# Deformable convolution before a state-space scan: the offset convolution in two halves, GpSimd's copies moved, output rows turned in the layer norm

## The reference, cut to what matters

```python
x = x + conv_ref(_gn(x), offset_w, offset_b, weight, bias)
t = _to_tokens(x)
t = t + ssm_ref(_ln_t(t), ...)
t = t + ffn_ref(_ln_t(t), ...)

def conv_ref(x, offset_w, offset_b, weight, bias):
    offsets = conv2d(x, offset_w, offset_b, PAD)          # 18 channels: dy and dx of 9 taps
    ys = (row - PAD) + kh + dy
    xs = (column - PAD) + kw + dx
    sampled = bilinear_sample(x, ys, xs)                  # a tap's value at a fractional place
    out = jnp.einsum('bkhwc,ock->bohw', sampled, w)
    return out + bias[None, :, None, None]
```

## Time and profile before

| | us |
|---|---|
| median of 3 executions | 323.08 |
| lowest, highest | 322.18, 323.83 |
| the profiled execution's own time | 324.19 |
| its span, first to last instruction | 322.4 |

### The profile page before, as it was taken

One profiled execution on the slowest core, in us unless ns is written; L12 is line 12 of the kernel. 1 busy time (PEld: TensorE's weight loads), 2 busy tenths in 40 slices (PEclk: granted clock), 3 DMA queues, 4 the chain that ended last, 5 costly groups with the idle time before them and its releaser, 6 DMA issues. The chain is left out here.

```text
span 322.4 us, 5895 instructions
## 1 busy us (share of the span) xinstructions
PE 254.4 (79%) x2341; PEld 149.2 (46%) x2341; DVE 245.2 (76%) x193; ACT 218.9 (68%) x327; POOL 170.1 (53%) x103
## 2 busy tenths in 40 slices
PE   7698999999797324387679666978599897888893
PEld 2345777776452000034347335644486764255530
DVE  0349999990458899999999999999999983216731
ACT  1047777776267749999999999999996442434541
POOL 1330000000184939999999999999998970000000
PEclk9988999999999555559875996597858999599998
DMA  5300000000003000000000000000000000000001
GB/s 164 129 0 2 2 0 2 2 2 2 0 18 81 0 18 0 1 2 0 2 1 2 2 2 0 0 3 2 1 2 2 2 2 0 3 19 0 0 0 33
DMA packets 2638, 4.07 MB, mean 13 GB/s; under 512 B 691, under 2 KB 1844, under 8 KB 2612
## 3 DMA queue, kind: packets, MB, share of 16 engines
q1 hardware_dynamic: 2480, 3.58, 3.8%
q10 hardware_dynamic: 132, 0.13, 0.1%
HBM read 2.66 MB, written 0.26 MB: 9 GB/s over the span
## 5 line engine op out<-in xcount | busy, mean ns | idle before, releaser
L830 DVE TENSOR_TENSOR_SCAN pool<-ps,pool 128x1024 f32<-128x1024 f32 x63 | 143.7, 2288 | 4.3 <-POOL pool L454 1.3
L454 POOL TENSOR_TENSOR pool<-pool 128x1024 f32<-128x1024 f32 x58 | 135.0, 2350 | 11.3 <-DVE pool L830 5.3
L1115 PE MATMUL ps<-pool,picks 96*128 96x512 bf16 x120 | 50.5, 515 | 45.3 <-DVE pool L830 45.3
L581 ACT ACTIVATE ps<-ps,a_cols 128x1020 f32<-128x1020 f32 x64 | 69.5, 1085 | 8.2 <-DVE pool L807 4.7
L571 ACT ACTIVATE pool<-ps 128x1024 f32<-128x1024 f32 x58 | 59.2, 1020 | 11.3 <-PE ps L1115 8.5
L516 ACT ACTIVATE pool<-ps 128x1024 f32<-128x1024 f32 x36 | 34.9, 1024 | 13.4 <-PE ps L1007 13.4
L279 DVE TENSOR_TENSOR pool<-pool 128x2048 f32<-128x2048 f32 x18 | 40.5, 2287 | 1.3 <-ACT pool L497 0.9
L1137 PE MATMUL ps<-pool 128*32 128x112 f32 x1024 | 39.6, 293 | 0.0
L417 POOL MEMSET pool<- 128x4096 f32 x1 | 3.5, 3512 | 68.2 <-DVE tn L719 68.2
L1115 PEld LDWEIGHTS ps<-pool,picks 96*128 96x128 bf16 x120 | 8.1, 109 | 67.2 <-DVE pool L830 65.6
L1137 PEld LDWEIGHTS ps<-pool 128*32 128x32 f32 x1024 | 30.7, 124 | 17.9 <-issue 17.9
(11 more groups left out here) (178 smaller groups left out, 257.2 us busy)
## 6 DMA issues: line engine op xcount, KB each, us to landing
pool<-ssm_w_dram SPq DMA_DIRECT2D x1, 896.0 KB, 9.2
pool<-pool SPq DMA_DIRECT2D x12, 64.0 KB, 2.0
pool<-offset_w_dram SPq DMA_DIRECT2D x1, 576.0 KB, 7.0
cst<-const_dram SPq DMA_DIRECT2D x1, 426.0 KB, 7.6
pool<-x_dram SPq DMA_DIRECT2D x2, 128.0 KB
pool<-conv_w_dram SPq DMA_DIRECT2D x1, 144.0 KB, 7.5
cst<-w_up_dram SPq DMA_DIRECT2D x2, 64.5 KB
cst<-w_attn_dram SPq DMA_DIRECT2D x2, 64.0 KB
```

The source lines that it names most:

```text
L454: pool_e.tensor_tensor(dbx[e % 3], bx, delta_wide[n % 2], ALU.mult).then_inc(pool_dbx_ready, 1)
L581: act.activation(decay[:, :, 1:HW], decay[:, :, 1:HW], ACT.Exp, scale=a_cols[:, PER * g + j:PER * g + j + 1]).then_inc(da_ready, 1)
L830: dve.tensor_tensor_scan(state[e % RING], slot(e), dbx[e % 3], 0.0, ALU.mult, ALU.add)\
L1115: ins = pe.matmul(slot(e)[:, column_half(c)], picks[:, j * 128:(j + 1) * 128], stack[0:96, g * SEQ + c * BANK:g * SEQ + (c + 1) * BANK], s ...
```

## The change

The offset convolution runs half by half, into banks 2 and 3; the filter groups move up by one bank, to banks 4 to 7. TensorE does half 0 with the first normalised half, filter group 0, the transposes of half 0, five taps of half 1, group 1, the other four taps, group 2, the transposes of half 1 and group 3. VectorE adds the grid by halves (`place_offsets`), the second half behind the first chunk, and makes the distances of round 1 behind the second chunk instead of the first. ScalarE makes the first hats ahead of groups 1 to 3, and those of round 1 behind the first chunk's copies. The sampling transposes wait for the last filter banks one by one instead of for all. The sum in bank 0 is opened by a zero matmul, the last tap sum closes it, and x is added by VectorE's last instruction. `turn_out_rows` moves into the first layer norm, in two parts, each in place of two of the four warming matmuls, and its copy on ScalarE behind the table load for Silu; the four warming matmuls ahead of the last filter group go. GpSimd's copies wait until the second distances are done (`hat_abs` at 2).

```diff
@@ -372,6 +371,8 @@
             pool_e.memset(eps[:, :], GN_EPS).then_inc(eps_set, 1)
             pool_e.memset(zero_bf[:, :], 0.0).then_inc(zero_set, 1)
             pool_e.memset(xpad, 0.0).then_inc(pad_zeroed, 1)
+
+            pool_e.wait_ge(hat_abs, 2)
             pool_e.wait_ge(spread_in, 16)
             pool_e.tensor_copy(picks[:, :].rearrange("p (j b d) -> p b j d", j=PER, b=HALVES),
                                spread[:, :].rearrange("p (b j) -> p b j", b=HALVES).unsqueeze(3)
@@ -487,7 +488,7 @@
                 half, side = divmod(n, 2)
                 for two in range(2):
                     act.wait_ge(z_done, 2 * n + two + 1)
-                    act.activation(zs[:, half, 2 * two:2 * two + 2, side, :], bank(3 + 2 * two, 2)
+                    act.activation(zs[:, half, 2 * two:2 * two + 2, side, :], bank(4 + 2 * two, 2)
                                    .rearrange("p (q k) -> p q k", q=2)[:, :, 0:TAPS * C], ACT.Copy).then_inc(z_ready, 1)
 
             def hats(i):
@@ -497,13 +498,9 @@
                 act.activation(v, v, ACT.Relu, bias=1.0, scale=-1.0).then_inc(hat_ready, 1)
 
             evacuate_filters(0)
-            evacuate_filters(1)
             hats(0)
-            evacuate_filters(2)
-            evacuate_filters(3)
-            act.wait_ge(rows_done, 1)
-            act.activation(out_rows[:, :], bank(0)[:, 0:(BATCHES + 1) * C], ACT.Copy).then_inc(rows_ready, 1)
-            hats(1)
+            for n in range(1, 4):
+                evacuate_filters(n)
 
             for it in range(HALVES * ROWS):
                 for j in range(3):
@@ -515,7 +512,7 @@
                         act.wait_ge(samp_turned, 6 * it + s + 1)
                         act.activation(sampT[j][:, 2 * side:2 * side + 2].rearrange("p q h n -> p (q h n)"),
                                        bank(2 + 2 * (s % 3), 2), ACT.Copy).then_inc(turned_ready, 1)
-                    if j == 0 and 0 < it < HALVES * ROWS - 1:
+                    if j == 0 and it < HALVES * ROWS - 1:
                         hats(it + 1)
 
 
@@ -528,6 +525,8 @@
 
             layer_norm(0)
             bring_in(ACT.Silu, 2)
+            act.wait_ge(rows_done, 1)
+            act.activation(out_rows[:, :], bank(3)[:, 0:(BATCHES + 1) * C], ACT.Copy).then_inc(rows_ready, 1)
             act.wait_ge(xs_done, 1)
             act.activation(xs, bank(4, 2), ACT.Copy).then_inc(xs_ready, 1)
             act.wait_ge(token_gate_in, 1)
@@ -677,9 +676,12 @@
             dve.wait_ge(const_in, 16)
             dve.tensor_reduce(blocks[:, :], ident.rearrange("p (m k) -> p m k", k=PLACES), AX.X, ALU.add)\
                .then_inc(blocks_ready, 1)
-            dve.wait_ge(off_done, 1)
-            dve.scalar_tensor_tensor(off, bank(2), part["offset_b"], part["grid"], ALU.add, ALU.add)\
-               .then_inc(off_ready, 1)
+
+            def place_offsets(half):
+                cols = slice(half * HW, (half + 1) * HW)
+                dve.wait_ge(off_done, half + 1)
+                dve.scalar_tensor_tensor(off[:, cols], bank(2 + half)[:, 0:HW], part["offset_b"], part["grid"][:, cols],
+                                         ALU.add, ALU.add).then_inc(off_ready, 1)
 
             def distances(i):
                 kk, half = divmod(i, HALVES)
@@ -693,17 +695,22 @@
                 dve.scalar_tensor_tensor(flat, flat, -1.0, flat, ALU.mult, ALU.max).then_inc(hat_abs, 1)
 
 
+            place_offsets(0)
             dve.wait_ge(offT_done, 1)
             distances(0)
             for it in range(HALVES * ROWS):
                 for j in range(3):
                     sampling_chunk(dve, it, j)
-                    if j == 0 and it + 1 < HALVES * ROWS:
+                    if it == 0 and j == 0:
+                        place_offsets(1)
+                    elif j == (it == 0) and it + 1 < HALVES * ROWS:
+                        if it == 0:
+                            dve.wait_ge(offT_done, 2)
                         distances(it + 1)
 
 
-            dve.wait_ge(conv_done, 1)
-            dve.tensor_scalar(t1[:, :], bank(0), part["conv_b"], None, ALU.add).then_inc(ln_in, 1)
+            dve.wait_ge(chunk_summed, 3 * HALVES * ROWS)
+            dve.scalar_tensor_tensor(t1[:, :], bank(0), part["conv_b"], xq, ALU.add, ALU.add).then_inc(ln_in, 1)
 
             def layer_norm(n, dst):
 
@@ -935,37 +942,44 @@
                 return slice(C * q, C * q + C)
 
 
-            def offset_taps(taps):
+            def offset_taps(half, taps):
                 for t in taps:
                     dy, dx = divmod(t, 3)
-                    ins = pe.matmul(bank(2), offw[:, t * 128:(t + 1) * 128], xpad[:, :, dy:dy + SIDE, dx:dx + SIDE],
-                                    start=t == 0, stop=t == TAPS - 1)
-                return ins
+                    ins = pe.matmul(bank(2 + half)[:, 0:HW], offw[:, t * 128:(t + 1) * 128],
+                                    xpad[:, half, dy:dy + SIDE, dx:dx + SIDE], start=t == 0, stop=t == TAPS - 1)
+                if t == TAPS - 1:
+                    ins.then_inc(off_done, 1)
+
+            def turn_offsets(half):
+                pe.wait_ge(off_ready, half + 1)
+                if half:
+
+                    pe.wait_ge(hat_diff, 1)
+                for t in range(2):
+                    c = 2 * half + t
+                    ins = pe.transpose(bank(1)[:, c * 128:(c + 1) * 128], off[:, c * 128:(c + 1) * 128], ident)
+                ins.then_inc(offT_done, 1)
 
             def filters(n):
 
                 half, side = divmod(n, 2)
                 for q in range(PAIRS):
-                    if n == 2 and q == 0:
-                        turn_out_rows()
-                    if n > 2 and q == 0:
-                        keep_warm(4)
                     if n and q % 2 == 0:
 
                         pe.wait_ge(z_ready, 2 * n - 1 + q // 2)
                     px = xn[quad(q), half * HW + side * 128:half * HW + side * 128 + 128]
-                    ins = pe.matmul(bank(3 + q)[:, 0:TAPS * C], px, convw[quad(q), :], start=True, stop=True)
+                    ins = pe.matmul(bank(4 + q)[:, 0:TAPS * C], px, convw[quad(q), :], start=True, stop=True)
                     if q % 2:
                         ins.then_inc(z_done, 1)
 
-            def turn_out_rows():
-
+            def turn_out_rows(batches):
                 pe.wait_ge(ssmw_in, 16)
                 pe.wait_ge(places_ready, 2 + BATCHES + 1)
-                for b in range(BATCHES + 1):
-                    ins = pe.matmul(bank(0)[:, b * C:(b + 1) * C],
+                for b in batches:
+                    ins = pe.matmul(bank(3)[:, b * C:(b + 1) * C],
                                     by_row[:, b * 128:(b + 1) * 128], wt["w_out"][:, 0:C], start=True, stop=True)
-                ins.then_inc(rows_done, 1)
+                    if b == BATCHES:
+                        ins.then_inc(rows_done, 1)
 
             def keep_warm(n, at=7):
 
@@ -976,27 +990,29 @@
             pe.wait_ge(zero_set, 1)
             keep_warm(20)
             pe.wait_ge(offw_in, 16)
-            pe.wait_ge(xn_ready, HALVES)
-            offset_taps(range(TAPS)).then_inc(off_done, 1)
+            pe.wait_ge(xn_ready, 1)
+            offset_taps(0, range(TAPS))
             pe.wait_ge(convw_in, 16)
             pe.wait_ge(xn_ready, HALVES + 1)
             filters(0)
 
             pe.wait_ge(const_in, 16)
-            pe.wait_ge(off_ready, 1)
-            for c in range(4):
-                ins = pe.transpose(bank(1)[:, c * 128:(c + 1) * 128], off[:, c * 128:(c + 1) * 128], ident)
-            ins.then_inc(offT_done, 1)
-            for n in range(1, 4):
-                filters(n)
-
-
-            pe.wait_ge(z_ready, 8)
+            turn_offsets(0)
+            offset_taps(1, range(5))
+            filters(1)
+            offset_taps(1, range(5, TAPS))
+            filters(2)
+            turn_offsets(1)
+            filters(3)
+            pe.matmul(bank(0), zero_bf[:, 0:128], zero_bf[:, :], start=True, stop=False)
 
             def turn(it, j):
                 pe.wait_ge(samp_made[j], it + 1)
                 for side in range(2):
                     s = 2 * j + side
+                    if it == 0 and 1 <= s < 3:
+
+                        pe.wait_ge(z_ready, 6 + s)
                     if 6 * it + s >= 3:
 
                         pe.wait_ge(turned_ready, 6 * it + s - 2)
@@ -1016,32 +1032,31 @@
                     for q in range(PAIRS):
                         ins = pe.matmul(bank(0)[quad(q), half * HW:(half + 1) * HW],
                                         zs[:, half, q, hh, k * C:(k + 1) * C],
-                                        sampT[j][:, q, hh, :], start=False, stop=False)
-                ins.then_inc(chunk_summed, 1)
+                                        sampT[j][:, q, hh, :], start=False, stop=(it, j, hh) == (HALVES * ROWS - 1, 2, 1))
+                return ins.then_inc(chunk_summed, 1)
 
```

(13 more changed lines are left out.)

3 lines of the change are left out of this document (1 added, 2 removed).

## The result

The changed kernel takes 320.4 us (median of four executions, 319.33 to 321.06) against 323.14 for the kernel before in the same comparison; the ratio is 0.9904, with a 95% interval of 0.9878 to 0.993. Predicted were 319.8, in a range of 317.3 to 321.5. The profiled execution took 321.06, 3.13 less than the profiled one of before; its span is 319.3 us.

What follows compares the result with a forecast made beforehand. TensorE was taken to bound the sampling loop at 2.90 per chunk, VectorE only 0.2 short. Last transposes -3.1, closing matmul -0.3, layer norm +0.1 gave -3.3: 323.08 to 319.8, own range 319.0 to 320.6, with rivals 317.3 to 321.5.

Steps and rivals of the forecast that it cites:

- Two halves and the order on TensorE: Start: halved convolution with interleaved TensorE work lets the first sampling transposes start at 22.5 instead of 27.68, -5.2 us.
- the rival with a doubled convolution: Offset convolution: a 256-column pass costs 0.43 as at full width, first sampling transposes at 30.0, 324 to 327 us; chance 0.04.
- the forecast's own sign of being wrong: Start: the forecast is wrong if, among other signs, filter evacuation holds TensorE past 22.5 us.
- VectorE becomes late: Sampling loop: VectorE's new order ends chunk 4 at 33.6 where TensorE wants it at 33.1, +0.5 us.
- Removed: TensorE: identity matmul that added x goes from the sampling loop, -0.8 us, and the closing zero matmul, -0.3 us.
- GpSimd's copies: Sampling loop: copies take strict turns with VectorE's two-operand multiplications on shared SBUF ports, last transposes at 73.6, +2.3 us.
- The rival that copies cost nothing: Sampling loop: one-operand copies don't take turns with multiplications; last transposes at 71.3, 317.5 us; chance 0.15.
- The rival that VectorE keeps the ports: Sampling loop: GpSimd only gets in during distances; last transposes at about 72.3, 318.5 us; chance 0.18.
- Layer norm: First layer norm: four of eight warming matmuls go and ten output-row passes come, +0.1 us, bounds 0 and 0.4.
- third rival: Layer norm: TensorE's clock falls to half rate under the projections behind it, +1.6, so 321.4 us; chance 0.14.
- A gain up to there passes on whole: Behind the first layer norm: what follows starts from its output, so time gained before it reaches the end in full.

Runs made afterwards that it cites:

- late copies: The changed kernel with GpSimd's copies held back until VectorE's last sampling multiplication, instead of until the second distances; 318.67 us, ratio 0.9855.

## Why the prediction was right, step by step

*Two halves and the order on TensorE* (-5.2): right, but 0.6 too large. The first turn came 4.83 earlier, 0.24 of it by x. A 256-column pass starts every 0.22 (18 in 4.12), as taken, so the rival with a doubled convolution falls. The distances start at 15.22 (15.4 foreseen, and x came 0.24 earlier). The last filter group ran from 21.40 to 22.70, its second pair waiting for ScalarE, as foreseen; but ScalarE emptied group 2 by 21.89 instead of 21.75, with x earlier. With that, about 0.4 of the 0.6 lies there. So the forecast's own sign of being wrong, a first turn held past 22.5 by the evacuation, came true by 0.35 (22.85).

*VectorE becomes late* (+0.5): here the delay of the first turn cancels. VectorE came as foreseen: with late copies chunk 4 ends at 33.12 (33.6 foreseen, x 0.41 earlier). But TensorE, 0.6 late at its first turn and still 0.4 late here, waits only 0.1: its turn starts at 33.18 where its own pace gives 33.08. So the delay of the first turn cost nothing, because this term was too large by as much.

*Removed* (-0.8, -0.3): right. From the first to the third turn it is 4.60 instead of 5.52 (27.68 to 33.20); the closing matmul's 0.29 is seen between the last tap sum's end (77.09) and VectorE's start (77.16), 0.07 against 0.36 in the earlier trace rows.

*GpSimd's copies* (+2.3): the mechanism is right, the size 0.5 too large. Shown by the late copies, which are free: 1.79. The term was mis-sized behind chunk 4, which was turned at 35.13 (35.4 foreseen, less x's 0.24: right). For the three chunks behind it VectorE was to need 9.2; it needed 8.69, from 35.07 to 43.76, which fits into TensorE's 8.70. The second copy of 0.6, priced at 0.4, ran beside the distances and cost nothing, and the 0.1 for each short copy is hidden once TensorE sets the pace. All 17 together cost 0.1, and the last turn came at 72.83 (73.6). The rival that copies cost nothing falls. The rival that VectorE keeps the ports is half right: short copies do wait out a whole multiplication, the long one got in behind the first and held the second.

The Trainium skill, "SBUF — State Buffer", section "SBUF: two separate sides", states the rule named here: a VectorE instruction with two SBUF inputs and a GpSimd instruction that reads SBUF lock one pair of ports, each for its whole length. The traces agree with its condition on both sides: multiplications beside memsets, which read nothing, stay at 4.49 for two, and a VectorE instruction with an operand in PSUM stays at 0.23 beside a GpSimd product. Who is next when both queue differed: beside the multiplications the two engines alternated, while seven short copies in a row held off one VectorE instruction for 1.45.

*Layer norm* (+0.1): 5.48 from the addition to the normalised tile in both kernels (77.16 to 82.64, and 81.31 to 86.79 before), so 0.0. That the clock may fall there (third rival) was right as a risk and was seen in four experiments, at 1.3 to 1.7; in the changed kernel's own profiled execution it held.

*"A gain up to there passes on whole"*: this statement failed. The last addition moved by 4.15, or 3.91 without x's earlier arrival, where the sum said 3.4; the end moved by 3.1. The first step of the decode took 0.61 of it and the scans 0.54. The total came out near the forecast because a stretch up to the last addition better by 0.5, x's 0.24 and a tail worse by 1.0 nearly cancel: 319.8 was partly luck.

The scans' 0.54 lies in three places, each two steps from scan to scan. Two are longer in the changed kernel, by 0.36 and 0.45, and one in the kernel before, by 0.28. The largest single step takes 2.61 (209.70 to 212.31) instead of 2.32 (213.13 to 215.45). ScalarE waits for a matmul ahead of it, GpSimd for ScalarE and the scan for GpSimd. TensorE's window and that matmul in the changed kernel, then in the kernel before:

```profile
206.70:209.70 3.00, 3.00 (x53) 0.65 0.02 5
...
207.75 1.03 PE L1130 MATMUL ps<-pool,picks 96*128 96x512 bf16 x2
```

```profile
210.13:213.13 3.00, 2.33 (x54) 1.00 0.04 8
...
210.71 0.61 PE L1115 MATMUL ps<-pool,picks 96*128 96x512 bf16 x2
```

All twelve profiled executions fit. This step takes 2.60 or 2.61 in the six whose TensorE had the half clock for 2.1 to 2.2 of the 3 us ahead of it, and 2.32 to 2.34 in the six with at most 1.4. The clock changes level many times during the scans in every kernel. What decides when stays open, as it does for the layer norm.

## What to carry to other kernels

When two engines share a port, price each meeting by the length of the instruction in between, and count only the meetings that delay the engine that sets the pace. Here one copy of 1.89 was nearly the whole price, and moving that copy alone won as much of the loop as moving all 18 (57.39 against 57.29), while seven copies of 0.5 cost 1.0. A wait that depends on where two instructions meet isn't removed by freeing one of them; look at the next instruction that can meet the same partner. And cut the trace at fixed events up to the end before saying that a gain passes on: in three of these kernels most of the 1 to 2 us won came back as a lower clock or as a held instruction.

## What the runs showed of the hardware that was not expected

- An instruction of 32 elements on one partition (0.24) can be held for 1.0 by a GpSimd product of 2.34, and is free with one operand in PSUM (0.23).
- In the two kernels in which TensorE stood longest between the first warming matmuls and the convolution (from 7.39 for 2.76 and from 7.90 for 3.26) the clock fell to half five passes into the convolution: 12.03 instead of 10.35 to the first multiplication. The eight others with the convolution in halves stood for 1.10 to 1.94 and kept 1.00. The kernel before stood for 2.73 and kept it too, so the wait alone does not decide.
- With two pairs of warming matmuls in the layer norm the granted clock fell there in the profiled executions of three kernels and held in those of five; with none it fell, and with four pairs it held in all three that have them, the kernel before among them. Each is one execution of its kernel.
